# Top-p attention kernel: a new order of the first attention step, adjacency products moved to the second step, and half of group 0's threshold passes moved from ScalarE to VectorE

## The reference, cut to what matters

```python
R = adj_like + eye ; R = R / R.sum(-1, keepdims=True)
for n in range(2):
    q, k = Xa @ W1.T @ W2.T, Xa @ W3.T
    p = softmax(q @ k.T)
    sp, cs = sorted descending p, cumsum(sp)
    A = p * (cs - sp < 0.9) ; A = A / A.sum(-1)
    Xf = R @ Xf
    Xa = A @ Xa
    Z  = Z + Xf @ U1[n].T + Xa @ U2[n].T
h = layer_norm(X + Z)
```

## Time and profile before

| | |
|---|---|
| median of 3 runs | 949.07 us (947.06 to 949.97) |
| the profiled execution, its own time | 950.71 us |
| its span in the trace | 949.0 us |
| busy: PE / DVE / ACT / POOL | 723.8 / 670.8 / 477.4 / 222.1 us |
| granted TensorE clock, mean | 0.889 of full |

### The profile page before, as it was taken

One profiled execution on the slowest core, in us unless ns is written; L12 is line 12 of the kernel. 1 busy time (PEld: TensorE's weight loads), 2 busy tenths in 40 slices (PEclk: granted clock), 3 DMA queues, 4 the chain that ended last, 5 costly groups with the idle time before them and its releaser, 6 DMA issues.

```text
span 949.0 us, 15349 instructions
## 1 busy us (share of the span) xinstructions
PE 723.8 (76%) x5090; PEld 532.7 (56%) x5091; DVE 670.8 (71%) x2313; ACT 477.4 (50%) x706; POOL 222.1 (23%) x477
## 2 busy tenths in 40 slices
PE   4999998779888176699999997675797796355284
PEld 2555554458777044587878765254675675345153
DVE  6758778614344456778885158799999999996868
ACT  4767776124444134353543376785685674721141
POOL 3302131505555250000000013214413413410000
PEclk9999999779999679899999998986988987777588
DMA  8753000346665300000000000000000001101001
GB/s 154 115 93 59 15 24 7 101 132 195 192 187 174 108 21 1 2 1 2 1 2 1 1 1 2 1 1 1 1 2 2 1 2 35 55 0 29 0 1 45
DMA packets 50437, 41.92 MB, mean 44 GB/s; under 512 B 7376, under 2 KB 48208, under 8 KB 50352
## 3 DMA queue, kind: packets, MB, share of 16 engines
q1 hardware_dynamic: 33136, 21.00, 7.9%
q0 software_dynamic: 11456, 14.62, 7.4%
q10 hardware_dynamic: 5760, 5.27, 2.1%
HBM read 39.69 MB, written 9.57 MB: 52 GB/s over the span
## 4 chain that ended last, share of the span: by engine, by line
DVE 29%; issue 26%; PE 5%; ACT 2%; POOL 2%; POOLq 1%; DVEq 1%; ACTq 0%
DVE cand L1378 3%; DVE big L1452 3%; DVE rm L1256 3%; DVE hacc L1373 2%; PE bank L1872 2%; DVE big L1443 2%; DVE big L1440 2%; DVE cand L1398 2%; DVE top L1393 1%; PE bank L2132 1%; PE bank L1937 1%; POOL res L1136 1%; POOL adjT L1134 1%; ACT xnT L1695 1%; PE bank L1956 1%
## 5 line engine op out<-in xcount | busy, mean ns | idle before, releaser
L1956 PE MATMUL bank<-ident,big 128*128 128x128 f32 x512 | 83.9, 316 | 38.4 <-DVEq L1482 32.7
L1707 ACT ACTIVATE big<-bank 128x512 f32<-128x512 f32 x128 | 70.9, 597 | 81.9 <-PE bank L1956 81.4
L1956 PEld LDWEIGHTS bank<-ident,big 128*128 128x128 f32 x512 | 65.1, 161 | 66.2 <-DVEq L1482 34.6
L1879 PE MATMUL bank<-parts,adjT 128*128 128x128 bf16 x1536 | 90.4, 221 | 2.3 <-DVE parts L1248 2.3
L1879 PEld LDWEIGHTS bank<-parts,adjT 128*128 128x128 bf16 x1536 | 88.8, 99 | 4.8 <-issue 4.6
L1872 PE MATMUL bank<-kk,qq 64*128 64x512 f32 x256 | 75.4, 714 | 13.8 <-ACT big L1680 13.8
L1452 DVE SCALAR_TENSOR_TENSOR big<-big,st 128x2048 f32<-128x2048 f32 x32 | 73.9, 2348 | 16.6 <-PE bank L1956 16.6
L1680 ACT ACTIVATE big<-bank,negm 128x2048 f32<-128x2048 f32 x32 | 62.6, 1957 | 44.6 <-DVE fsc L1486 40.5
L1148 POOL TENSOR_SCALAR bt<-bt 128x1 f32<-128x1 f32 x16 | 6.3, 396 | 333.3 <-ACT big L1697 208.0
L365 POOL DMA_INDIRECT ys_scratch<-big,parts x62 | 60.2, 971 | 64.6 <-ACT big L720 49.6
L600 DVE TENSOR_TENSOR big<-big,bank 128x512 f32<-128x512 f32 x31 | 21.3, 687 | 64.1 <-ACT big L738 44.1
(11 more groups left out here) (349 smaller groups left out, 1484.4 us busy)
## 6 DMA issues: line engine op xcount, KB each, us to landing
big<-in_L_ffn_w_dram SPq DMA_DIRECT2D x93, 128.0 KB
big<-in_adj_dram POOLq DMA_DIRECT2D x8, 512.0 KB, 7.4
big<-xs_scratch ACTq DMA_DIRECT2D x31, 132.0 KB
kk<-in_adj_dram POOLq DMA_DIRECT2D x4, 512.0 KB, 8.3
qq<-in_adj_dram POOLq DMA_DIRECT2D x4, 512.0 KB, 10.1
big<-ys_scratch SPq DMA_DIRECT2D x8, 256.0 KB, 5.0
xs_scratch<-hacc SPq DMA_DIRECT2D x9, 132.0 KB
xs_scratch<-hacc ACTq DMA_DIRECT2D x8, 132.0 KB
```

Source lines behind the costliest of these rows:

```text
L1707: nc.scalar.activation(MT[:, 4 * q:4 * q + 4, s * P:(s + 1) * P], bank[:, 5 + q % 2, :].rearrange("p (j i) -> p j i", j=4), ACT.Copy).then ...
L1879: mm = nc.tensor.matmul(bank[:, b, i * P:(i + 1) * P], adjT[:, jt, t * P:(t + 1) * P], parts[:, k, jt, :], start=(jt == 0 and k == 0), sto ...
L1956: mm = nc.tensor.transpose(bank[:, 5 + q % 2, j * P:(j + 1) * P], mk[:, s, jt * P:(jt + 1) * P], ident[:, :])
```

## The change

The change has these parts:

- Step 0, DVE: `group(0, 0)` now begins after `rest(1)`; the remaining `third` and `rest` stand inside it, behind V. In each group `row_max(0, g + 1, 0)` stands between V and the masks and `row_max(0, g + 1, 1)` after the flags: only the next group's maxima. The rounds over the candidates wait for a semaphore of their own (c_ready) and the factor of Z comes after them.
- Step 0, ACT: for each g first `take_pv(g - 2)`, then the eight mask copies, then both exponentials of group g + 1. Step 0, PE: `logits(0, g + 1, 0)` behind the first two sets of transposes, `logits(0, g + 1, 1)` behind `pv(0, g - 1, 0)`; `rx_first` is gone from the rounds; `turn_x` and keys of the next step are spread over rounds 3, 5 and 7.
- Adjacency: `rx_first(0)` does two tiles; the other fourteen are done in step 1, five pairs near its beginning and two in round 1. `less_w` runs in rounds 2 and 3 of step 1, and `rx` in rounds 4 to 7. The sum is kept in `xnT` from tile 2 on, with one copy each on DVE and ACT.
- Group 0's thresholds: the four Sign passes go from ACT to DVE as counts (`count`, four passes with a sum over 2048 columns), with waits of POOL for them. For g > 0 all the waste of ACT's passes goes to one buffer, so each pass waits for the pass before it.
- The fourth block: three semaphores are merged into others.

```diff
-        WT = [(0, 1, 2)] + [(2 + g,) for g in range(1, NG)] + [(10, 11), (12, 13), (14, 15)]
-        WU = [4] * NG + [4, 7, 4]
-        RXG = (2, 2, 3, 3, 4, 4, 5, 5)
+        WU = [4, 4, 7, 4, 7, 4, 4, 4]
+        RXG = (4, 4, 5, 5, 6, 6, 7, 7)
 # POOL
-                    pool.wait_ge(tried, 4 * g + (s + 3 if g else 2 * s + 2))
+                    pool.wait_ge(tried, tries(g, s, 1) + (2 if g else 1))
...
+                        pool.wait_ge(counted, 2 * s + 2)
 # DVE
+                def count(s, k):
+                    dve.wait_ge(p_ready, NG * G + s + 1)
+                    if k:
+                        dve.wait_ge(found, 2 * s + 1)
+                    nc.vector.tensor_scalar(mk[:, 1, :], prob[:, 0, s, :], bt[:, B_T2, s:s + 1] if k else first[:, 0:1],
+                                            None, ALU.is_lt, ALU.add, accum_out=bt[:, 2 * k + B_S1, s:s + 1]
+                                            ).then_inc(counted, 1)
 # in group(n, g)
-                                take_w(NG + 1 + s)
+                                if s == 0:
+                                    count(1, 1)
+                                take_w(1 + s)
...
-                    if n == 0 and g + 1 < NG:
-                        row_max(n, g + 1, 1)
+                    if n == 0 and g == 0:
+                        third(1)
+                        for q in range(2, NC):
+                            rest(q)
+                            third(q)
+                    if n == 0 and g + 1 < NG:
+                        row_max(n, g + 1, 0)
+                    if n and g < 2:
+                        take_w(6 if g else 3)
...
+                        if g == 0:
+                            take_w(4)
...
-                    if g + 2 < NG:
-                        row_max(n, g + 2, 0)
-                    if n == 0:
-                        take_w(g)
+                    if n == 0 and g + 1 < NG:
+                        row_max(n, g + 1, 1)
+                    if n and g + 2 < NG:
+                        row_max(n, g + 2, 0)
+                    if n == 0 and g == 0:
+                        take_w(0)
+                    if n and g == 0:
+                        take_w(5)
+                    if n and g == 1:
+                        take_w(7)
 # DVE, beginning of step 1
+                count(0, 0)
+                row_max(n, 0, 1)
                 for p in range(2):
                     xa_quad(p)
-                row_max(n, 0, 1)
+                count(0, 1)
+                count(1, 0)
+                row_max(n, 1, 0)
                 for p in range(2, NC):
                     xa_quad(p)
-                row_max(n, 1, 0)
-                take_w(NG)
 # ACT
+                    if g:
+                        act.wait_ge(tried, tries(g, s, k))
...
+                    if g:
+                        act.wait_ge(tried, tries(g, s, k) + 1)
+                        nc.scalar.activation(waste1, prob[:, b, s, :], ACT.Sign, bias=t, scale=-1.0,
+                                             accum_out=bt[:, 2 * k + B_S1, s:s + 1]).then_inc(tried, 1)
 # PE, a round of step 0
+                for g in range(1, NG):
+                    turn_mk(0, g - 1, range(2))
+                    if g + 1 < NG:
+                        logits(0, g + 1, 0)
+                    else:
+                        pe.wait_ge(p_ready, NG * G)
+                        make_kk(1, 0)
+                    turn_mk(0, g - 1, range(2, 4))
...
+                    turn_mk(0, g - 1, range(4, 8))
+                    if g % 2 and g > 1:
+                        turn_x(1, g // 2 - 1)
+                    pv(0, g - 1, 0)
+                    if g + 1 < NG:
+                        logits(0, g + 1, 1)
+                    else:
+                        pe.wait_ge(c_xT_a, 2 + 3)
+                        make_kk(1, 2)
...
                     flag_sum(g)
+                    pv(0, g - 1, 1)
 # PE, beginning of step 1
                 logits(1, 0, 0, ready1)
...
+                logits(1, 0, 1)
                 for p in range(2):
                     u_quad(p)
-                logits(1, 0, 1)
+                logits(1, 1, 0)
                 for p in range(2, NC):
                     u_quad(p)
-                logits(1, 1, 0)
-                rx_first(NG)
-                rx_first(NG + 1)
+                rx_first(1)
                 logits(1, 1, 1)
-                rx_first(NG + 2)
-                for j in range(3):
-                    less_w(0, j)
+                rx_first(2)
+                rx_first(3)
+                rx_first(4)
                 logits(1, 2, 0)
-                for j in range(3):
-                    less_w(1, j)
+                rx_first(5)
                 flag_sum(NG)
 # PE, rounds of step 1
+                    if g == 1:
+                        rx_first(6)
...
+                    if g == 1:
+                        rx_first(7)
+                    if g in (2, 3):
+                        for j in range(3):
+                            less_w(g - 2, j)
```

More of the change, by code:

```diff
@@ L1493, in _ @@
                 rest(1)
-                row_max(0, 1, 0)
-                third(1)
-                for q in range(2, NC):
-                    rest(q)
-                    third(q)
                 for g in range(NG):
@@ L1532, in _ @@
                     group(n, g)
-                    if g >= 2:
-                        stats_of(g - 2)
-                stats_of(NG - 2)
+                    for k in range(NG - 1):
+                        if RXG[k] == g:
+                            stats_of(k)
                 ch.sync()
@@ L1593, in _ @@
                 v = op(nc.vector.max_index(idx8[:, :], r8[:, M8, :], r8[:, EX8, :]))
[L1594 removed]
+                nc.vector.tensor_tensor(one[6], r8[:, M8, 1:2], r8[:, M8, 0:1], ALU.subtract).then_inc(d_nm, 1)
                 since(v)
@@ L1655, in take_xT @@
                     act.wait_ge(c_xT, n * NC + c + 1)
-                    nc.scalar.activation(chunk_of(xnT, c), bank[:, c, :], ACT.Copy).then_inc(c_xT_a, 1)
+                    nc.scalar.activation(chunk_of(xnT, c), bank[:, 4 if n else c, :], ACT.Copy).then_inc(c_xT_a, 1)
                 def take_kk(n, c):
@@ L1678, in exp @@
                     if n == 0:
-                        nc.scalar.activation(cand[:, b, s, :], cand[:, b, s, :], ACT.Exp, bias=negm[:, b, s:s + 1])
+                        nc.scalar.activation(cand[:, b, s, :], cand[:, b, s, :], ACT.Exp, bias=negm[:, b, s:s + 1]
+                                             ).then_inc(c_ready, 1)
                     nc.scalar.activation(prob[:, b, s, :], bank[:, 0:4, :].rearrange("p b n -> p (b n)"), ACT.Exp,
@@ L1730, in take_part @@
                         nc.scalar.activation(parts[:, j, q * TPC:(q + 1) * TPC, :].rearrange("p t d -> p (t d)"),
-                                             bank[:, WB[half][i], :], ACT.Copy).then_inc(sp_part, 1)
+                                             bank[:, WB[i], :], ACT.Copy).then_inc(sp_part, 1)
                 def take_pv(g):
@@ L1746, in _ @@
                 second(1)
+                take_ab(3)
+                second(2)
+                second(3)
                 for g in range(NG + 1):
-                    if g + 1 < NG:
-                        exp(0, g + 1, 0)
-                    if g == NG:
-                        for c in range(3):
-                            take_xT(1, c)
+                    if g >= 2:
+                        take_pv(g - 2)
                     if g:
@@ L1779, in _ @@
                 exp(1, 0, 0)
-                for p in range(2):
-                    take_u(p)
                 act.wait_ge(c_id, NT + 1)
@@ L1784, in _ @@
                 exp(1, 0, 1)
-                for p in range(2, NC):
+                for p in range(2):
                     take_u(p)
@@ L1789, in _ @@
                 exp(1, 1, 0)
+                for p in range(2, NC):
+                    take_u(p)
                 below(0, 1, 1)
-                below(1, 0, 0)
-                exp(1, 1, 1)
-                take_part(0, 0)
-                below(1, 1, 0)
-                take_part(0, 1)
-                take_part(0, 2)
-                below(1, 0, 1)
-                take_part(1, 0)
-                below(1, 1, 1)
-                take_part(1, 1)
-                take_part(1, 2)
-                for g in range(1, NG + 1):
-                    if g + 1 < NG:
+                act.wait_ge(u_done, 2 * NC)
+                nc.scalar.activation(xnT[:, 3 * CH:], hacc[:, 3 * TPC:, :].rearrange("p t d -> p (t d)"), ACT.Copy
+                                     ).then_inc(u_act, 1)
+                for g in range(NG + 1):
+                    if g and g + 1 < NG:
                         exp(1, g + 1, 0)
-                    for k in range(4 * G):
-                        copy_MT(1, g - 1, k)
+                    if g:
+                        for k in range(4 * G):
+                            copy_MT(1, g - 1, k)
                     if g + 1 < NG:
@@ L1822, in _ @@
```

(9 more changed lines are left out.)

181 lines of the change are left out of this document (92 added, 89 removed).

## The result

The change made the kernel faster. Over four runs on one chip the kernel after had a median of 925.64 us (923.25 to 928.30) and the kernel before, beside it, 949.52 us; the ratio is 0.974, with a 95% interval of 0.967 to 0.980. The forecast was 923.5 us, with a range of 913 to 936. Between the medians the change is worth 23.9 us, where 25.6 were forecast from 949.07.

The account below looks back on a forecast made before the run. PE was taken to bound step 0 and DVE step 1. Terms of -8.5, -15.2, -2.4, -3.0, +1.2 and +2.4 sum to -25.5 us: 950.71 becomes 925.2, with the median 1.6 lower, forecast 923.5 us, range 913 to 936.

Parts of the forecast that it names:

- What bounds: PE is full in step 0 and DVE in step 1, so moved PE work goes to an engine with gaps.
- 1, opening of step 0: Start of step 0 up to group 0's m_ready: candidate rounds begin behind rest(1), a gain of 8.5 us.
- 2, six rounds: Six rounds of step 0: DVE bounds at 16.65 us each, 103.5 with charges against 118.7, a gain of 15.2 us.
- Rival B: Step 0's round is a loop of PE and ACT, 18.1 us each: +9, 932.5 us; chance 0.22.
- 3, end of step 0: From group 6's transposes to the end of pv(0,7,1): 29.5 us against 31.85, a gain of 2.4 us.
- 4, opening of step 1: End of pv(0,7,1) to first m_ready of step 1: 68.4 us against 71.3, a gain of 3.0 us.
- Rival A: Group 0's counts on DVE run at double rate, 1.15 us less for each: 920 us; chance 0.17.
- Rival C: Adjacency tiles moved into step 1's opening are on the path, m_ready at 78: +10, 933.5 us; chance 0.12.
- 5, rounds of step 1: Rounds of step 1: +1.2 us for two take_w, +2.4 for less_w in two rounds, 0 for moved adjacency tiles.
- rival D: ACT's passes in step 1 wait for themselves, at 1.6 us a wait: +28, 951.7 us, slower than before; chance 0.03.
- The sum: All terms together: -25.5 us from the profiled 950.71, giving 925.2, and a forecast median of 923.5 us.

Follow-up runs that it names:

- tiles_back: The kernel after with one adjacency tile put back into each of rounds 1 to 7 of step 0, new order kept: 923.17 us, ratio 0.990.
- old_light: The kernel before with the adjacency tile of rounds 1 to 7 of step 0 cut to 1 of 48 matmuls, old order kept: 928.27 us, ratio 0.995.
- open_back: The kernel after with third and rest of the later quarters put back ahead of group 0 on DVE: 907.34 us, ratio 0.973.
- control: The kernel after, unchanged, run again beside follow-up kernels on another chip: 908.62 us, ratio 0.975 to the kernel before there.
- swap: The kernel after with logits(1,1,1) ahead of rx_first(1) on PE: 902.79 us, ratio 0.968.
- less_spread: The kernel after with the three steps of each less_w spread over the round and take_part moved with them on ACT: 903.67 us, ratio 0.970.
- no_count: The kernel after with group 0's Sign passes back on ACT and no counts on DVE: 903.30 us, ratio 0.968.

## Why the prediction was right, step by step

**What bounds.** Right: PE was full in step 0, as tiles_back shows (2.6 us a round for a tile of 2.84). But the sentence that one moves PE work from a full engine to one with gaps tells half: by old_light the move alone is worth 0.6 us in the six rounds and 4.3 in the whole step. The prediction had the right round since it worked out one in which both halves were done; it did not say how little either half gives alone. The expectation of 109 us for old_light had the old order's wait right and left out the clock.

**1, opening of step 0.** Predicted 8.5, measured 7.9, of which 0.5 the other way stand ahead of the stage (negm 360.27 and 360.80), so 8.4 within it. The part of it that is third and rest is 2.4 by open_back; the prediction did not split it, and the expectation of 3.7 was too high, since only 2.63 us of idle time stood there to be filled. rx_first(0) was put at 5.5 us and at no cost; it took 7.15 in the control, and DVE's second maximum waited 0.24 us for the logits behind it.

**2, six rounds.** Predicted 103.5, measured 100.3. DVE's own round was read as 16.65; they took 18.43 and then 16.55, 16.57, 16.47, 16.47, 16.46. The first was cold as said, but 1.8 us late, not 2.3; the charges of 0.4 and 0.9 for turn_x and the load did not come. The other rounds were 0.15 shorter each, and the transposes followed a by 1.8 us in group 0 and by 1.1 in group 6. Together this term was mis-sized by 3.2 us. Rival B is out: PE's tie with DVE held at 0.30 us of slack, with waits of 0.19 to 0.20 us ahead of the masks in three of the later rounds.

**3, end of step 0.** 28.5 for 29.5.

**4, opening of step 1.** 68.4 us to m_ready, predicted 68.4, and tile 1 at 40.3 behind the end of pv, predicted 39.9. The counts take 2.35 us each, which is 1.15 ns a column where the slope of the earlier trace rows gave 1.0 and the prediction took 2.27 us. By the Trainium skill, "VectorE: DVE Perf Modes", section "The perf-mode tier table", a scalar operation on fp32 in SBUF would take about half of that, 1227 ns. The table has no entry for one with a sum, and the trace shows that its figure does not carry over to that one: 2.35 us. Rival A is out with it. Rival C is out: the pairs of tiles of rx_first take the full clock's 5.5 us but for one, which takes 6.88 behind 3.23 us of idle time, and the first flag product is on time; but rx_first(1) did hold DVE, by 2.45 us (swap), which the prediction had charged.

**5, rounds of step 1.** Here a term failed in size. less_w was charged 1.2 us in each of two rounds; the traces show waits of 2.80 and 2.30, and less_spread wins 2.6 and 2.4 back. The error of judgment was in the choice between the bounds 0 and 5.4, by the thought that half a chain costs a quarter of the wait; the chain waits on ACT's turns, 2.97 us in one piece, and its matmuls take up to twice as long where the clock is low. The term has no single size, though. In the six traces with the chain in one piece the two waits come to 5.1 (after), 5.1 (control), 3.7 (no_count), 2.3 (tiles_back), 2.3 (open_back) and 1.9 us (swap); the 2.4 of the prediction lies within that span, and the two traces of the kernel after at its upper end. The two take_w (+1.2, measured +0.9) were right. ACT's passes take 2.12 us from start to start; in the kernel before, without that wait, they take 1.98 (592.25 and 594.23). So waiting on its own last pass costs 0.14 us, where the prediction read 0.13 from the earlier trace rows:

```profile
592.79 1.99 ACT L1746 ACTIVATE UT<-big,first 128x2048 int8<-128x2048 f32 x1
594.91 2.00 ACT L1750 ACTIVATE UT<-big,first 128x2048 int8<-128x2048 f32 x1
...
618.48 1.97 ACT L1730 ACTIVATE big<-bank,negm 128x2048 f32<-128x2048 f32 x1 [6.60 <-DVE fsc L1537]
```

The next exponential still has 6.60 us of idle time ahead of it, so rival D is out. The move of the adjacency tiles was charged 0. The two last rounds became 1.3 and 1.7 us longer (33.12 to 34.43, 30.62 to 32.34), as add_rx came into them; the rounds that end in groups 2 and 3 grew by only 1.35 and 1.34 (37.04 to 38.39, 36.55 to 37.89) although their waits are 2.80 and 2.30, as add_rx left them. With -0.4 and 0 in the two rounds between, the move comes to some 0.4 us (6.3 less 0.9 and 5.0); it was not tested alone.

**The sum.** -25.5 predicted, -26.3 measured between the two profiled executions, -23.9 between the medians. Terms 2 and 3 were 4.2 us better than charged and term 5 2.7 worse, with 0.6 in term 1: the errors happen to cancel, and it is luck that the total is closer than its parts.

## What to carry to other kernels

When two engines alternate in a round, ask of each piece of work what wait it now covers: removing a piece pays only if the order no longer leaves that wait, and a new order pays only if there is no longer work in the place. Build the round of the changed kernel in full, engine by engine, before pricing the parts, since the parts did not add up here (in the six rounds 0.6 and -1.2 alone, 14.3 together; over step 0 4.3 and 11.4 alone, 30.2 together). A short chain between two engines that stands ahead of a hand-over is better spread over the round than left in one piece.

## What the runs showed of the hardware

- With less work PE's granted clock fell: with a tile of 2.84 us taken out of each round it went from 0.97 to 0.91 over the six rounds. Behind one and the same wait of 1.69 us the logits took 3.54, 3.34 and 3.67 us in three rounds and 1.99 in two.
- The same chain of code cost DVE 2.80 us or nothing, and the matmuls of that round differed by PE's granted clock (1.00 and 0.62 in the chain). In this kernel a change below about 3 us can be made or undone by it in a stage far away.
- An operation on POOL over one column took 2.33 us, where the same line took 0.19 at 526.55, while DVE ran a pass of 2.35 us with two tensor inputs, the same tile twice (L1407), at 537.05:

```profile
537.12 2.33 POOL L1161 TENSOR_SCALAR bt<-bt 128x1 f32<-128x1 int32 x1 [0.15 <-issue]
```

- The counts, which read one tensor, did not do that: an operation of POOL at 532.62, beside a count (531.07 to 533.42), took 0.21 us.
